# Layer 1 attention: row sums by accumulating exponentials, maxima to rows by transpose and DMAs, a new order of the items

## The reference, cut to what matters

```
q, k = xn @ q_w + q_b, xn @ k_w + k_b
att = softmax(q . k over 32 channels + mask, over the keys)
y = att @ ((xn @ v_w + v_b) * mask)
h = silu(layer_norm(y) * (1 + scale) + shift) @ out_w + out_b
x + h
```

## Time and profile before

| | us |
|---|---|
| median of 3 runs | 1376.7 (1375.37 to 1378.49) |
| span of the profiled execution | 1373.9 |
| time of the profiled execution beside its span | not listed; the span is 2.8 below the median |
| PE, weight loads, DVE, ACT, POOL busy | 1333.1, 1059.5, 1014.5, 782.5, 747.4 |

### The profile page before, as it was taken

How to read it: one execution, slowest core, us unless ns; L and a number is a source line. 1 busy time by engine, 2 the same in 40 slices (tenths; PEclk the granted TensorE clock), 3 DMA queues, 4 the chain that set the end, 5 groups by cost and what they waited for, 6 DMA issues and landing times.

```text
span 1373.9 us, 28281 instructions
## 1 busy us (share of the span) xinstructions
PE 1333.1 (97%) x10936; PEld 1059.5 (77%) x10936; DVE 1014.5 (74%) x2004; ACT 782.5 (57%) x1357; POOL 747.4 (54%) x674
## 2 busy tenths in 40 slices
PE   8999999999999899999999999999999999999998
PEld 5778888888888787677777777777777777777666
DVE  5887978788787877678757857857857856856855
ACT  5455455454545563756756755765765765765663
POOL 0323243432333433548947957956966965965832
PEclk9999999999999999999999999999999999999999
DMA  9011111312113356846546546556456456454512
GB/s 340 35 43 62 39 64 37 100 31 70 62 39 93 93 184 200 246 124 185 160 118 178 154 132 178 143 143 177 135 152 172 129 156 161 140 153 140 157 30 93
DMA packets 83303, 173.44 MB, mean 126 GB/s; under 512 B 7624, under 2 KB 7624, under 8 KB 83168
## 3 DMA queue, kind: packets, MB, share of 16 engines
q1 hardware_dynamic: 83168, 171.62, 42.3%
HBM read 104.45 MB, written 67.14 MB: 125 GB/s over the span
## 4 chain that ended last, share of the span: by engine, by line
PE 71%; DVE 13%; ACT 7%; DMA 3%; SPq 2%; issue 2%; POOL 1%; DVEq 0%; ACTq 0%
PE ps L546 13%; PE ps L548 12%; PE ps L547 12%; PE ps L722 8%; PE ps L775 8%; PE ps L705 8%; DVE cT L1253 4%; PE ps L541 4%; PE ps L727 2%; ACT Qs L963 2%; ACT xTh L835 2%; ACT ps L837 2%; DVE ps L1220 1%; PE ps L655 1%; PE ps L634 1%
## 5 line engine op out<-in xcount | busy, mean ns | idle before, releaser
L1441 POOL TENSOR_TENSOR Pb<-Pb 128x512 f32<-128x512 f32 x360 | 449.9, 1291 | 209.5 <-PE ps L775 209.3
L1253 DVE TENSOR_REDUCE cT<-ps 128x1 f32<-128x512 f32 x512 | 324.4, 681 | 110.9 <-PE ps L705 108.6
L986 ACT ACTIVATE Pb<-ps 128x512 f32<-128x512 f32 x512 | 285.3, 600 | 210.8 <-PE ps L722 203.5
L722 PE MATMUL ps<-Qs,Ks 106*128 106x512 f32 x512 | 197.1, 419 | 6.4 <-DVE xTl L1105 3.3
L705 PE MATMUL ps<-Ks,Qs 98*128 98x512 f32 x512 | 185.2, 413 | 4.1 <-DMA Ks<-stack_scratch 1.0
L1365 POOL TENSOR_TENSOR rs<-ve,mhalf 128x4 f32<-128x4 f32 x32 | 33.0, 1031 | 216.9 <-DVE ve L1073 158.4
L722 PEld LDWEIGHTS ps<-Qs,Ks 106*128 106x128 f32 x512 | 95.5, 189 | 52.2 <-issue 12.4
L705 PEld LDWEIGHTS ps<-Ks,Qs 98*128 98x128 f32 x512 | 96.9, 191 | 47.0 <-DVE cT L1253 15.5
L546 PE MATMUL ps<-xTh,Wh_k 128*128 128x512 f32 x256 | 106.9, 418 | 5.9 <-DVE xTl L1105 3.0
L546 PE MATMUL ps<-Wh_o,sTh 128*128 128x512 f32 x256 | 106.8, 417 | 2.1 <-DVE sTl L1231 2.1
L546 PE MATMUL ps<-Wh_v,xTh 128*128 128x512 f32 x256 | 103.1, 403 | 0.0
(11 more groups left out here) (180 smaller groups left out, 2968.1 us busy)
## 6 DMA issues: line engine op xcount, KB each, us to landing
Qs<-stack_scratch SPq DMA_DIRECT2D x32, 768.0 KB
Ks<-stack_scratch SPq DMA_DIRECT2D x32, 768.0 KB
stack_scratch<-sg_q SPq DMA_DIRECT2D x32, 512.0 KB, 2.7
stack_scratch<-sg_k SPq DMA_DIRECT2D x32, 512.0 KB, 2.7
wr<-in_x SPq DMA_DIRECT2D x32, 256.0 KB, 4.8
x_scratch<-wr SPq DMA_DIRECT2D x32, 256.0 KB, 2.0
stack_scratch<-sg_q SPq DMA_DIRECT2D x32, 256.0 KB, 3.1
stack_scratch<-sg_k SPq DMA_DIRECT2D x32, 256.0 KB, 3.4
```

The costliest lines, as they stand in the source:

```text
L722: e.matmul(bank[:], Ks[par][0:RE, j, m * 128:(m + 1) * 128], Qs[par][0:RE, j, :], start=True, stop=True).then_inc(s["ST"], 1)
L986: e.activation(p_buf(n, m)[:, j, :], ps[bank_of["a", n, m, j]][:], ACT.Exp).then_inc(s["P"], 1)
L1253: e.tensor_reduce(nx[:, n % 2, j, t, 0:1], ps[bank_of["S", n, j, t]][:], AX.X, ALU.max, negate=True).then_inc(s["S_max"], 1)
L1441: e.tensor_tensor(acc[:, j, :], acc[:, j, :], p_buf(n, m)[:, j, :], ALU.add).then_inc(s["Ps_pool"], 1)
```

## The change

- Row sums: ACT now also takes the exponential of each bank of S in place, with the negated maximum as bias, and accumulates its sum into `dn` (`S` on ACT). The bank is free after that (`done` by `S_exp`). POOL's additions, `den`, `dl` and the sums' transpose go; `divisors` takes reciprocals of `dn`.
- Maxima to rows: after DVE's three reductions a DVE transpose (in blocks of 32x32) of the 128x128 tile, then eight DMAs of SP, four blocks times high and low part, each from four partitions of nxT to one row of Qs in pieces of 32 values. Rows 98 and 99 of Qs hold them against ones in Ks, so the matmuls of `a` have 100 rows. `a` waits for all eight.
- `pv`: one block a step, with four P buffers, one for each key block; that of step n - 1 stands in step n. The queries are in natural order, and `pv` reads P with a stride; x is loaded by one DMA.
- Seven banks rotate. Normalisations of layer 1 (`nx`, `ny`, except two tiles of the last) move from ACT to POOL.
- PLAN, all of it, layer 0's part too, has new positions.

```
-RM, RX, RE = 96, 98, 106
+RM, RX, RE = 96, 98, 100
 EARLY = 12
+PVB = 7
...
-    "S": (0.216,), "nxt": (1.2, 0.3, 0.0),
-    "a": (0.216,), "pv": (2.0,), "den": (0.9,), "dl": (2.0,), "ae": (0.0,),
-    "tl": (0.3,), "tle": (0.5, 0.5), "tlx": (0.1, 0.3, 0.4, 0.4, 0.4, 0.4),
-    "stacks": (0.0,), "kset": (0.5, 0.5), "ones": (0.0,), "ahead": (0.0,), "narrow": (0.0,), "end": (0.0,),
+    "S": ((0.422, 0.55, 0.742, 0.811, 0.898), (0.396, 0.525, 0.936, 1.048, 1.099), (0.477, 0.9, 1.006, 1.108, 1.192), (0.066, 0.069, 0.727, 0.814, 0.999)),
+    "a": (0.216,), "pv": (4.0,),
+    "tl": (0.3,), "tle": (0.5, 0.5), "tlx": (0.3, 0.4, 0.4, 0.4, 0.4),
...
-    "att": ((0.154, 0.267, 0.392, 0.584, 0.736), (0.002, 0.187, 0.345, 0.514, 0.66), (0, 0.298, 0.519, 0.672, 0.873), (0, 0.275, 0.306, 0.45, 0.581)),
-    "pv": ((0.365, 0.753, 0.853), (0.338, 0.788, 0.924), (0.466, 1.021, 1.054), (0.328, 0.788, 0.957)),
-    "S": ((0.405, 0.414, 0.494, 0.654, 0.71), (0.151, 0.37, 0.491, 0.614, 0.834), (0.186, 0.206, 0.601, 0.645, 0.677), (0.211, 0.351, 0.417, 0.515, 0.783)),
+    "0k": ((0.157, 0.58), (0.489, 0.551)),
+    "att": ((0.053, 0.062, 0.082, 0.233, 0.461), (0.01, 0.088, 0.245, 0.401, 0.741), (0.093, 0.109, 0.262, 0.692, 0.887), (0.349, 0.494, 0.559, 0.616, 0.645)),
+    "pv": ((0.043,), (0,), (0,), (0.041,)),
+    "tl": (None, (0.467, 1.131), (0.214, 0.217), (0.603, 0.7)),
+    "tlx": ((0.277, 0.483), None, None, None),
+    "ty": ((0, 0.854, 1.112), (0, 0.98, 1.049), (0, 1.11, 1.155), (0, 1.13, 1.169), (1, 0.038, 0.177)),
+    "S": ((0.422, 0.55, 0.742, 0.811, 0.898), (0.396, 0.525, 0.936, 1.048, 1.099), (0.477, 0.9, 1.006, 1.108, 1.192), (0.066, 0.069, 0.727, 0.814, 0.999)),
+    "nxt": ((0.923, 1.15), (1.106, 1.131), (1.173, 1.2), (1.183, 1.186)),
+    "q": ((0.103, 0.141, 0.49), (0, 0, 0.086), (0.018, 0.115, 0.135), (0.049, 0.185, 0.238)),
+    "k": ((0.527, 0.575, 0.782), (0.051, 0.192, 0.44), (0.243, 0.573, 0.583), (0.163, 0.432, 0.506)),
+    "stack": ((1.2, 1.2), (0.696, 0.806), (0.756, 0.999), (0.602, 0.932)),
+    "nx": (None, (0.075, 0.301), None, None),
+    "tx": (None, (1.2, 1.2), None, None),
+    "o": ((1, 0.4, 0.549), (1, 0.617, 1.158), (1, 0.953, 1.2), (2, 0.655, 1.019)),
+    "v": ((2, 0.972, 1.157), (3, 0.498, 0.668), (3, 0.646, 0.993), (3, 0.95, 1.02)),
+    "1t": ((0.23, 0.233), (0, 0.311), (0.021, 0.282), (0, 0), (0.274, 0.374), (0.272, 0.301), (0.364, 0.541), (0.698, 0.773), (0.389, 0.592), (0.334, 1.141), (0.738, 0.816), (1.003, 1.2), (1.019, 1.15), (0.283, 0.781)),
+    "lx": ((0.254, 1.043), None, None, None),
+    "lr": ((0.321, 0.774), None, None, None),
...
-        put("pv", [("pv", n, 0), ("pv", n, 2), ("ae", n)])
+        if n:
+            put("pv", [("pv", n - 1)])
         if n and g:
             put("tl", [("tl", n - 1)])
         if n and g == 0:
-            put("tlx", [("tl", n - 1), ("den", n - 1), ("tlx", b - 1), ("ny", 8 + b - 1)])
+            put("tlx", [("tl", n - 1), ("tlx", b - 1), ("ny", 8 + b - 1)])
...
-            put("dl", [("dl", n - 1, 2), ("dl", n, 0)])
-        if n + 2 == N1:
-            put("dl", [("dl", n, 0)])
...
-            top = 6
+            top = PVB
...
+        dn = sb("dn", [128, 2, NT, H1])
         nx = cT[:].rearrange("p a b -> p (a b)").rearrange("p (n j t s) -> p n j t s", n=2, j=4, s=2)
-        nxs = sb("nxs", [128, RM + 10 * NT], FR)
+        nxs = sb("nxs", [128, NT, 32], FR)
+        nxT = sb("nxT", [128, NT * 32])
...
-        Pb = [sb(f"Pb{i}", [128, 4, T]) for i in range(3)]
+        Pb = [sb(f"Pb{i}", [128, 4, T]) for i in range(NT)]
...
-                return s["S_max"], 16 * key[1] + 4 * key[2] + key[3] + 1
-            if k == "nxt":
-                return s["nxq"], 2 * key[1] + 2
...
-            def nxt(i, n):
-                if i == 1:
-                    bank = take(("nxt", n))
-                    e.wait_ge(s["nx_lo"], n + 1)
-                    for t in range(NT):
-                        r = e.matmul(bank[0:RE, t * 128:(t + 1) * 128], nxs[:, 10 * t:10 * t + RE], identr[:],
-                                     start=True, stop=True)
-                    r.then_inc(s["nx_tr"], 1)
-
             def a(i, n, m, j):
                 par = n % 2
                 bank = take(("a", n, m, j))
-                if m == 0 and j % 2 == 0:
-                    e.wait_ge(s["nxq"], 2 * n + 1 + j // 2)
+                if m == 0 and j == 0:
+                    e.wait_ge(s[f"nxq{par}"], 128 * (n // 2 + 1))
                 e.matmul(bank[:], Ks[par][0:RE, j, m * 128:(m + 1) * 128], Qs[par][0:RE, j, :],
                          start=True, stop=True).then_inc(s["ST"], 1)
 
-            def sums(p, h, first, last):
-                for u in range(4):
-                    r = e.matmul(DEN[32 * u:32 * u + 32, 0:128], sel[:, H1 - 1 - h:H1 + 31 - h], p[:, 128 * u:128 * u + 128],
-                                 start=first, stop=last)
-                return r
-
-            def den(i, n):
+            def pv(i, n):
                 b, g = divmod(n, NG)
-                e.wait_ge(s["Ps_pool"], ps_count(n, 3, 3))
-                if n == 0:
-                    e.wait_ge(s["sel"], 2)
-                    if bank_before["bank", 7] is not None:
-                        e.wait_ge(*done(bank_before["bank", 7]))
-                elif g == 0:
-                    e.wait_ge(s["dT"], b)
-                for j in range(4):
-                    h = 4 * g + j
-                    r = sums(p_buf(n, 0)[:, j, :], h, h == 0, h == H1 - 1)
-                r.then_inc(s["den"], 1)
-
-            def dl(i, n, first):
-
-                if n == N1 - 1 and first == 0:
-                    e.wait_ge(s["dT"], B)
-                for m in (first, first + 1):
-                    e.wait_ge(s["P"], 16 * n + 4 * m + 4)
-                    for j in range(4):
-                        h = 4 * (n % NG) + j
-                        r = sums(p_buf(n, m)[:, j, :], h, m == 0 and h == EARLY, m == 3 and h in (EARLY - 1, H1 - 1))
-                r.then_inc(s["den"], 1)
-
-            def pv(i, n, first):
-
-                b, g = divmod(n, NG)
-                if first == 0 and g and n < N1 - 1:
-                    den(0, n - 1)
-                for m in (first, first + 1):
+                for m in range(NT):
                     e.wait_ge(s["P"], 16 * n + 4 * m + 4)
                     if m == 0:
                         if n == 0:
-                            if bank_before["bank", 6] is not None:
-                                e.wait_ge(*done(bank_before["bank", 6]))
+                            if bank_before["bank", PVB] is not None:
+                                e.wait_ge(*done(bank_before["bank", PVB]))
                         else:
                             e.wait_ge(s["y1"], n)
                         if g == 0:
                             e.wait_ge(s["v_hi"], 4 * (8 + b) + 4)
-                    pb = p_buf(n, m)
                     for j in range(4):
                         h = 4 * g + j
                         for u in range(4):
                             r = e.matmul(PV[32 * u:32 * u + 32, 128 * j:128 * j + 128], xbuf(8 + b)[:, m, h * 32:(h + 1) * 32],
-                                         pb[:, j, 128 * u:128 * u + 128], start=(m == 0 and j == 0),
+                                         t4(Pb[m][:, j, :])[:, :, 32 * u:32 * u + 32], start=(m == 0 and j == 0),
                                          stop=(m == NT - 1 and j == 3))
                     r.then_inc(s["PV"], 1)
...
-                if i > 4 and (x > 8 or (x == 0 and i % 2 == 1)):
+                if i > 4 and x == 0 and i % 2 == 1:
...
-                if i > 4 and x >= 8 and not (x == 15 and i % 2 == 0):
+                if i > 4 and x == 15 and i % 2 == 1:
...
-            def nxt(i, n):
-                if i == 2:
-                    rows = ps[bank_of["nxt", n]][RM:RE, :].unsqueeze(1).to_broadcast([RE - RM, 2, T])
-                    e.wait_ge(s["nx_tr"], n + 1)
-                    for h in range(2):
-                        e.copy(Qs[n % 2][RM:RE, 2 * h:2 * h + 2, :], rows).then_inc(s["nxq"], 1)
+            def S(i, n, j, t):
+                b, g = divmod(n, NG)
+                if g == 0 and j == 0 and t == 0 and b >= 2:
+                    e.wait_ge(s["rd"], b - 1)
+                e.wait_ge(s["S_max"], 16 * n + 4 * j + t + 1)
+                bank = ps[bank_of["S", n, j, t]]
+                e.activation(bank[:], bank[:], ACT.Exp, bias=nx[:, n % 2, j, t, 0:1],
+                             accum_out=dn[:, b % 2, t, 4 * g + j:4 * g + j + 1]).then_inc(s["S_exp"], 1)
 
             def a(i, n, m, j):
-                if n == 0 and j == 0 and m < 3:
-                    e.wait_ge(*((s["w_lo"], w_end(1, "q")), (s["q_tr"], 32), (s["y_mm"], 64))[m])
-                if m == 3:
-                    if j == 0:
-                        e.wait_ge(s["PV"], 4 * n + 2)
-                    if n < N1 - 2:
-                        e.wait_ge(s["Ps_pool"], ps_count(n, 1, j))
```

(90 more changed lines are left out.)

147 lines of the change are left out of this document (46 added, 101 removed), and 10 rows, old and new, of the table PLAN.

## The result

The changed kernel takes 1431.9 us (median of 4 runs, 1424.9 to 1434.3) against 1376.2 for the kernel before: a ratio of 1.0389, with a 95% interval of 1.0350 to 1.0428. The forecast was 1344 us in a range of 1316 to 1393, so the time lies outside the range and on the other side of no change.

What follows compares the result with a forecast made beforehand. PE was taken as the bound, with an image falling from 104.6 to 100.2 us. Seven images x 4.4 = 30.8, + 5 (last image) - 2 (entry) - 1 (layer 0) = 33; 1373.9 - 33 + 2.8 gives 1344 us, range 1316 to 1393.

Steps and rivals of the forecast that it cites:

- eight DMAs on SP, which starts DMAs 0.37 apart, so 8 x 0.37 = 3.0: Maxima to rows, each step of layer 1: issuing the eight row DMAs takes SP 3.0 us.
- the landing: Arrival of the row pieces after their issue: taken as 2.0 us, between bounds of 2.0 and 11.3.
- the forecast's own chain of 6.6: From the last S matmul to the first transposed-score matmul: 0.7 + 0.6 + 0.3 + 3.0 + 2.0 = 6.6 us, against about 3.7 before.
- In two of four steps I charge 1 us each: PE's wait for rows: value block (3.7) plus projections or tails cover 5.8 to 7 us, leaving 2 us an image.
- What waits behind them is at most an output store: SP's queue: stack loads stand ahead of the row DMAs or behind them, so at most an output store is delayed.
- A pair of exponential and accumulator read: ACT's added work on S: 0.70 us a pair, 64 pairs, 44.8 us an image.
- some 50: Sign of a right forecast: PE's busy time down by some 50 us.
- The walk's "about 2" for S in g = 0: PE waiting for ACT to free S banks in an image's first step: about 2 us.
- the entry: Start of layer 1: the first rows take 6.6 us, covered only by what is left of o and v; 2 us lost.
- Rival 2: First transposed score of each step: ACT idles at the hand-over and becomes the bound; slower, 1394 us; chance 0.22.
- Rival 5: Row DMAs land like loads, 11.3 us instead of 2.0, once an image; slower, 1409 us; chance 0.03.
- Rival 3: PE has room and untouched waits decide; image stays 104.6 us, 1375 in all; chance 0.07.

Runs made afterwards that it cites:

- four_dmas: Changed kernel with the high and low part of a block in one row DMA, four a step instead of eight: 1362.1 us, ratio 0.9895.
- cover: Changed kernel with the q and k projections of the g = 0 step moved ahead of its first transposed score: 1421.5 us, ratio 1.0329.
- warm8: Changed kernel with unused matmuls (20, 2, 6, 6 in the four steps) filling PE's waits for the rows: 1420.3 us, ratio 1.0322.
- four_nosexp: Four row DMAs a step, and ACT's exponentials of S left out, against four_dmas: 1349.0 us, ratio 0.9808.
- no_sexp: Changed kernel, eight row DMAs kept, without ACT's exponentials of S (divisors a constant): 1429.7 us, ratio 1.0387.
- split4: four_dmas with two of the four row DMAs issued by ACT instead of SP: 1395.8 us, ratio 1.0158.
- mix4: four_dmas with two row DMAs issued by POOL, but all four by SP in steps with g = 1: 1360.9 us, ratio 0.9890.
- pool4: four_dmas with two row DMAs issued by SP and two by POOL in every step: 1418.1 us, ratio 1.0309.
- stride4: four_dmas with layer 1's token order turned: 512-byte pieces, P read contiguously, S weights loaded with stride four, x by four DMAs: 1364.9 us, ratio 0.9919.

## Why the prediction was wrong

**The step that failed** is "eight DMAs on SP, which starts DMAs 0.37 apart, so 8 x 0.37 = 3.0". The starts are 0.67 apart, and eight take 5.3 to 5.7 us. I took the distance of two stores to DRAM for a DMA between two SBUF tiles, without bounds, and bounded only the landing, which was right (1.9 against 2.0). The chain is 8.6 us and not 6.6.

**A second step failed beside it, and would have without it: the cover.** "In two of four steps I charge 1 us each" took 5.8 to 7 us of PE's work as cover in each step. In g = 0 there was nothing but the value block of 3.70 us: even the forecast's own chain of 6.6 leaves a wait of 2.9 there, and with 8.6 it is 4.97. four_dmas, with a chain of 5.7 (845.70 - 840.66, and 0.68), still waits 2.05. Over the span PE waits 54.3 us for rows instead of the 16 that I charged.

**What came behind the waits.** "What waits behind them is at most an output store" was false: the next step's stack loads do, for 8.4 us. ACT stands idle in the same waits and has its exponentials afterwards (cover). The clock falls behind them, which costs at least 9 to 12 us (warm8). I had no price for either of the last two. That the row DMAs and what follows from them make up most of the loss is shown as a whole: with half of them 70 of the 88 us between forecast and time are back. How the 70 divides among the waits for rows, the late stack loads, ACT and the clock was measured only in part, by warm8 and by the lists of waits; the rest stays open.

**What held.** A pair of exponential and accumulator read took 0.66 us (forecast 0.70); ACT 93.45 us an image (91.3 to 97.6); the value block 3.70 with strided reading (3.7); DVE and POOL are covered; the first exponential of P comes at 537.8 against 534.3 (the forecast: 3 later). PE's busy time fell by 11 us and not by some 50, as records at the lower clock are longer; with four DMAs it fell by 30. The walk's "about 2" for S in g = 0 doesn't come out of its own terms (11.2 - 6.5 - 4.7 is 0); PE's waits for ACT in a steady image are 1.5 us at four DMAs, so that term was nearly right by luck. With four DMAs, whose starts of 2.7 us come nearest to the 3.0 I had assumed, the steady image is 101.9 us where I had 100.2. The first image is longer, 108.9 at a granted clock of 0.92, with PE waiting 4.7 us in it for S banks that ACT frees late; I had priced it like the others, though before it was 1 us shorter than they (103.5). The forecast's sum leaves 730.8 - 30.8 = 700.0 for seven images, 100.0 each. Against that the first takes 8.9 more and the five between 1.6 each; the seventh (108.7) and the last (100.5, forecast 103.8) take 5.4 more together, and the entry is 2.5 less. That is the 20 us by which the span of 1360.9 stands above the forecast's 1340.9. Without the exponentials of S (four_nosexp) the first image has a clock of 0.97 and takes 104.2 us, and the seventh 102.0, so about half of the 20 lies with the coupling of PE and ACT in these two.

**The last image** was to win 5 us. From its first exponential of P to the end it takes 106.8 us (1432.2 - 1325.4) against 108.8 before, so 2; with four DMAs it is 100.5, so 8.

**The rivals.** Rival 2 has the place and the shape of what came: ACT idles at the hand-over, and the time ends above before. Its point was 3.3 us of idle a step; in g = 0 it was 7.86. But its cause (ACT as the bound) is refuted at eight DMAs by no_sexp, and its price of 1394 was for 4 us of idle a step. Rival 5 had rows that come late, by landing instead of starting. Rival 3 had the image stay at 104.6: at four DMAs it is 101.9, which fits PE's work counting, though PE's work was not varied alone.

## What to carry to other kernels

Price the issue of a DMA by a row of the same kind of DMA, and where there is none, bound it upward as well as the landing; several small DMAs in a row on one queue are a serial chain of starts. Put into one DMA what its access pattern can hold: here a change from eight to four turned 3.9% slower into 1.05% faster than the kernel before (four_dmas). Ask of a hand-over what both coupled engines do in it, and what the issuing queue has next. Read the cover of each step from the order by itself: here one step of four had 3.70 us of it where 5.8 to 7 were assumed.

## What the runs showed of the hardware

The start of a small SBUF-to-SBUF DMA on SP cost 0.62 us, with 0.65 to 0.67 between starts (0.70 in pairs beside another queue), with 8, 16 or 32 pieces and with pieces of 128 or 512 bytes. ACT's pairs took 1.33 us (split4) and POOL's 1.24 to 1.32 (mix4, pool4). The stores of the same traces start 0.36 to 0.39 apart on SP. A read of the accumulator moves the next ACT instruction by 0.09 us, though its own record is 0.23 long. A moving operand read in runs of 32 values was as fast as a contiguous one (3.70 us for a value block with the one and, in stride4, with the other). With a stationary operand loaded with a stride of four values the kernel took 1364.9 us against 1362.1, with intervals that overlap.
